# Third-norm parts of six late row blocks: stored in the attention stage, loaded for their products

## The reference

```
x = x + 0.5 * ffn(layernorm(x))
x = x + attention(layernorm(x))
x = x + 0.5 * ffn(layernorm(x))

def ffn(x):                       # x: tokens x 1024
    dots = softmax(x @ centroids.T / 0.1)          # 64 clusters
    hits = dots > 0.01
    query_sel, cluster_sel = any(hits, axis=1), any(hits, axis=0)
    dense = x @ weight.T + bias                    # 1024 x 1024
    return where(query_sel[:, None] & cluster_sel[assignments][None, :], dense, 0)
```

## Time and profile before

| | us |
|---|---|
| median of 3 runs | 1193.3 (1192.45 to 1193.41) |
| profiled execution, its own time | 1196.15 |
| its span | 1194.3 |
| TensorE busy | 1181.7 (99%) |
| VectorE busy | 799.3 (67%) |
| ScalarE busy | 499.2 (42%) |
| GpSimd busy | 441.0 (37%) |

### The profile page before, as it was taken

The page is one execution under the profiler, slowest core; times in us unless marked ns, Lnnn a source line. Parts: engine busy times, 40 slices in busy tenths (PEclk is TensorE's granted clock), DMA queues, the critical chain, the costliest instruction groups (busy, mean ns, idle before and its releaser), DMA issues.

```text
span 1194.3 us, 24986 instructions
## 1 busy us (share of the span) xinstructions
PE 1181.7 (99%) x10072; PEld 1002.5 (84%) x10072; DVE 799.3 (67%) x1272; ACT 499.2 (42%) x718; POOL 441.0 (37%) x582
## 2 busy tenths in 40 slices
PE   7999999999999999999999999999999999999998
PEld 6888888888888888888888888888888878888887
DVE  6654554455444477787777877778777774199987
ACT  5232233222211355656656656565565663211110
POOL 1335445543424643433434334344343210051332
PEclk9999999999999999999999999999999999999999
DMA  8578777876565366565565666565655565017885
GB/s 275 144 206 232 207 206 193 225 211 182 164 189 159 98 169 169 148 171 146 160 166 139 181 152 152 160 155 164 161 142 164 129 169 193 2 72 259 279 304 195
DMA packets 344978, 208.73 MB, mean 175 GB/s; under 512 B 289440, under 2 KB 308640, under 8 KB 344864
## 3 DMA queue, kind: packets, MB, share of 16 engines
q1 hardware_dynamic: 329696, 187.73, 56.2%
q10 hardware_dynamic: 15168, 19.40, 4.7%
HBM read 118.49 MB, written 88.60 MB: 173 GB/s over the span
## 4 chain that ended last, share of the span: by engine, by line
PE 91%; DMA 3%; DVE 2%; issue 1%; ACT 1%; SPq 1%; POOL 1%; POOLq 0%; DVEq 0%
PE ps_b L285 9%; PE ps_q L285 8%; PE ps_q L287 8%; PE ps_q L286 8%; PE ps_b L287 8%; PE ps_b L286 8%; PE ps_a L285 8%; PE ps_a L287 8%; PE ps_a L286 8%; PE ps_t L292 6%; PE ps_q L1450 3%; PE ps_q L299 2%; PE ps_q L301 2%; PE ps_q L1425 2%; DMA y_scratch<-xa 1%
## 5 line engine op out<-in xcount | busy, mean ns | idle before, releaser
L318 POOL TENSOR_TENSOR var_eps<-moments,eps 128x1 f32<-128x1 f32 x96 | 18.2, 190 | 396.6 <-DVE moments L314 396.6
L285 PE MATMUL ps_a<-w_hi,odd_hi 128*128 128x512 f32 x368 | 147.7, 401 | 0.0
L287 PE MATMUL ps_a<-w_hi,odd_lo 128*128 128x512 f32 x368 | 143.8, 391 | 0.0
L286 PE MATMUL ps_a<-w_lo,odd_hi 128*128 128x512 f32 x368 | 143.2, 389 | 0.0
L635 POOL TENSOR_SCALAR f_out<-f_out,token_on 128x1024 f32<-128x1024 f32 x30 | 85.6, 2852 | 75.6 <-DVE f_out L1013 75.3
L686 POOL TENSOR_TENSOR x_ring<-x_ring,f_tmp 128x1024 f32<-128x1024 f32 x32 | 77.3, 2414 | 91.2 <-DVE best L1159 58.5
L285 PE MATMUL ps_b<-proj_hi,y_hi 128*128 128x512 f32 x256 | 103.3, 403 | 0.0
L287 PE MATMUL ps_b<-proj_hi,y_lo 128*128 128x512 f32 x256 | 100.0, 391 | 0.0
L286 PE MATMUL ps_b<-proj_lo,y_hi 128*128 128x512 f32 x256 | 99.7, 390 | 0.0
L327 ACT ACTIVATE y_tok<-x_ring,norms 128x1024 f32<-128x1024 f32 x64 | 79.7, 1245 | 38.0 <-ACT o_head L881 21.0
L737 POOL TENSOR_TENSOR late<-late,mask 128x1024 f32<-128x1024 f32 x18 | 44.1, 2463 | 137.3 <-DMA late<-x_scratch 91.6
(11 more groups left out here) (219 smaller groups left out, 3113.1 us busy)
## 6 DMA issues: line engine op xcount, KB each, us to landing
xa<-in_L_attn_x SPq DMA_DIRECT2D x32, 512.0 KB, 5.0
f_tmp<-f_scratch SPq DMA_DIRECT2D x32, 512.0 KB, 4.2
x_ring<-in_L_attn_x SPq DMA_DIRECT2D x32, 512.0 KB, 3.6
f_scratch<-f_out SPq DMA_DIRECT2D x30, 512.0 KB, 4.0
x_scratch<-x_ring SPq DMA_DIRECT2D x30, 512.0 KB, 3.5
y_scratch<-xa SPq DMA_DIRECT2D x28, 512.0 KB, 4.6
ya_tok<-y_scratch SPq DMA_DIRECT2D x112, 128.0 KB, 3.3
late<-x_scratch SPq DMA_DIRECT2D x22, 512.0 KB, 6.7
```

The source lines that it names most:

```text
L285: pe.matmul(acc, hi[:, k, :], w_h[:, k, cols], start=(k == 0), stop=False)
L286: pe.matmul(acc, hi[:, k, :], w_l[:, k, cols], start=False, stop=False)
L287: last = pe.matmul(acc, lo[:, k, :], w_h[:, k, cols], start=False, stop=(k == KB - 1))
```

## The change

Six late blocks, v = 3, 5, 7, 9, 11 and 13 (blocks 9, 13, 17, 21, 25 and 29), are no longer normed, turned and split in the late stage. Their high and low parts, which the attention stage makes anyway for the logits, are stored to a new scratch tensor there, and loaded into the places of `late_set` in the late stage, after the block that used the place before. The semaphores count turned blocks (`TURNED`: v = 1, 2, 4, 6, 8, 10, 12) instead of all. x2 of the loaded blocks is still loaded, as the residual.

```diff
+    LOADED = list(range(3, len(LATE), 2))
+    TURNED = [v for v in range(1, len(LATE)) if v not in LOADED]
+    parts_d = nc.dram_tensor("parts_scratch", (len(LOADED), 2, P, KB, P), F32, kind="Internal").ap()
...
+        parts_stored, parts_in = w_in[6], [w_in[7], assign_in]
...
+                def store_parts(v):
+                    sp.wait_ge(lo3, LATE[v] + 1)
+                    for n, part_of in enumerate(third_set(LATE[v])):
+                        sp.dma_start(parts_d[LOADED.index(v), n], part_of.bitcast(F32)).then_inc(parts_stored, 16)
...
                     if 0 <= i - 4 < NT - 2:
                         store_x2(i - 4)
+                    if i - 5 in LATE[1:] and LATE.index(i - 5) in LOADED:
+                        store_parts(LATE.index(i - 5))
...
+                def load_parts(v):
+                    n = LOADED.index(v)
+                    sp.wait_ge(parts_stored, 32 * n + 48)
+                    for h in range(2):
+                        sp.wait_ge(ffnl[h], v - 2)
+                    for m, part_of in enumerate(late_set(v)):
+                        sp.dma_start(part_of.bitcast(F32), parts_d[n, m]).then_inc(parts_in[n % 2], 16)
...
                     if 7 <= v + 4 < NL:
                         load_late(v + 4)
+                    if v + 3 in LOADED:
+                        load_parts(v + 3)
...
                 def high_third(t):
                     act.wait_ge(t3, t + 1)
+                    if t - 2 in LATE[1:] and LATE.index(t - 2) in LOADED:
+                        act.wait_ge(parts_stored, 32 * LOADED.index(LATE.index(t - 2)) + 48)
                     act.copy(third_set(t)[0], ps_t[:, :, :]).then_inc(hi3, 1)
...
                 for v in range(3, NL):
-                    high_late(v)
+                    if v in TURNED:
+                        high_late(v)
                     if v == 3:
                         store_late(0)
-                    if v + 1 < NL:
+                    if v > 3 and v + 1 in TURNED:
                         norm_late(v + 1)
...
-                    if v > 0:
-                        dve.wait_ge(yl, v)
+                    if v in LOADED:
+                        dve.wait_ge(late_in[(v - 1) % 6], 16 * ((v - 1) // 6 + 2))
+                    elif v > 0:
+                        dve.wait_ge(yl, TURNED.index(v) + 1)
...
-                low_late(3)
                 for v in range(1, NL):
                     if v > 1:
                         read_late(v - 1, 1)
                         add_late(v - 1, 1)
-                        if 4 < v + 1 < NL:
+                        if v + 1 > 4 and v + 1 in TURNED:
                             low_late(v + 1)
...
+                    elif v in LOADED:
+                        n = LOADED.index(v)
+                        pe.wait_ge(parts_in[n % 2], 32 * (n // 2) + 48)
                     else:
-                        pe.wait_ge(lol, v)
+                        pe.wait_ge(lol, TURNED.index(v) + 1)
...
                 for v in range(2, NL):
-                    if v + 1 < NL:
+                    if v + 1 in TURNED:
                         transpose_late(v + 1)
                     product_late(v, 0)
                     product_late(v, 1)
```

More of the change, by code:

```diff
@@ L860, in norm_late @@
                         act.wait_ge(heads, NT)
-                    wait(act, tl, v - 2)
-                    normed(act, late_y[v % 2][:, :], late_slot(v)[:, :], 2, LATE[v]).then_inc(yl, 1)
+                    n = TURNED.index(v)
+                    wait(act, tl, n - 1)
+                    normed(act, late_y[(n + 1) % 2][:, :], late_slot(v)[:, :], 2, LATE[v]).then_inc(yl, 1)
                 def high_late(v):
-                    act.wait_ge(tl, v)
+                    act.wait_ge(tl, TURNED.index(v) + 1)
                     act.copy(late_set(v)[0], ps_t[:, :, :]).then_inc(hil, 1)
@@ L956, in _ @@
                 high_late(2)
-                norm_late(3)
+                norm_late(4)
                 select_mask(act, 1)
@@ L1098, in low_late @@
                     hi, lo = late_set(v)
-                    dve.wait_ge(hil, v)
+                    dve.wait_ge(hil, TURNED.index(v) + 1)
                     dve.tensor_tensor(lo, ps_t[:, :, :], hi.bitcast(F32), ALU.subtract).then_inc(lol, 1)
@@ L1393, in transpose_late @@
                 def transpose_late(v):
-                    pe.wait_ge(yl, v)
-                    if v == 1:
+                    n = TURNED.index(v)
+                    pe.wait_ge(yl, n + 1)
+                    if n == 0:
                         pe.wait_ge(lo3, NT)
                     else:
-                        pe.wait_ge(lol, v - 1)
-                    transposes(pe, late_y[v % 2]).then_inc(tl, 1)
+                        pe.wait_ge(lol, n)
+                    transposes(pe, late_y[(n + 1) % 2]).then_inc(tl, 1)
                 def product_late(v, h):
```

## The result

The change made the kernel slower: 1196.77 us at the median of 17 runs (1193.66 to 1200.05) against 1194.09 of 17 runs before (1192.45 to 1198.01), a ratio of 1.0024 with an interval of 1.0015 to 1.0032. The forecast was 1187.4 us. The profiled execution has a span of 1197.5 us, 3.2 more than that of before.

What follows compares the result with a forecast made beforehand. TensorE was taken to bound the kernel: 5.4 us of turns and 0.45 us of VectorE's lateness give 5.9 us less than 1193.3, so 1187.4 us, range 1186.3 to 1190.9 us.

Steps and rivals of the forecast that it cites:

- What bounds the kernel: Whole kernel: TensorE's instruction stream, busy 1181.7 of 1194.3 us, sets the end, with VectorE 0.45 us behind it.
- What the turns are worth: Late stage: six turns leave TensorE at 0.90 us each, 5.4 us in all, plus 0.45 us of VectorE's lateness.
- The attention stage taken at nothing: Attention stage: the stores of parts fit into SP's 4.7 us wait before the x load, so they cost nothing.
- rival C: Gain eaten: late stage at 1192.6 us, or attention stage losing 1 us in six steps; 1191 to 1195 us, chance 0.10.
- rival D: Attention stage: stores delay loads leading to q and k; slower from 1.4 us per pair, 1202 us at 2.5; chance 0.07.
- price of the pieces: DMA time of parts moved in 512-byte pieces: 1.5 to 2.5 us per 512 KB.
- Does the streamed chain hold?: Late stage: the streamed blocks' cycle falls from 23.59 to 22.0 us, under TensorE's new 22.67 us.
- the next one or two streams: Late stage: part loads delay only these streamed loads, by up to 3 us, with 2.4 us in hand.
- Which VectorE makes up in the following block: Late stage: the delay of up to 3 us is recovered through VectorE's shorter wait for the mask.
- B: Late stage: the streamed chain becomes the bound because the DMA engines need over 22.67 us; likely 1189.6 us, chance 0.20.
- the signs that I had set for being wrong: End chain running through streamed loads, or 512-byte pieces costing more than 2.5 us per 512 KB.
- the DMA share of the late blocks: Late stage, profile after: DMA engines' busy share over two late blocks at 0.95 or more.

Runs made afterwards that it cites:

- run without transfers: Kernel before with six late blocks neither turned nor loaded, no stores or loads of parts, so wrong numbers are multiplied: ratio 0.9951 to before, 5.8 us faster.
- products ahead: The change with parts laid out in 4 KB runs and each streamed block's product loaded one step before its x2: ratio 0.9953 to before, 5.6 us faster.
- late half alone: The change without stores of parts, its late loads taking other data of the same size: ratio 0.9995 to the kernel before.
- stores-only kernel: Kernel before plus only the attention stage's twelve stores of parts in 512-byte pieces and their guarding wait: ratio 1.0044 to before, 5.2 us slower.
- stores twice: Kernel before plus only the stores of parts in 512-byte pieces, each part stored two times: ratio 1.0189 to before, 22.6 us slower.
- whole rows: The change with the two places of the parts one after the other, so 4 KB runs instead of 512 bytes: ratio 0.9978 to before, 2.6 us faster.
- all three edits: The change with 4 KB runs, product parts loaded one step ahead, and stores of parts issued before the x2 store: ratio 0.9961 to before.

## Why the prediction was wrong
**What bounds the kernel**: right. TensorE's stream set the end but for 0.45 us, and the two things to watch were named.

**What the turns are worth**, 5.4 us and 0.45 more: right. The run without transfers has 5.8.

**The attention stage taken at nothing**: this step failed. I followed what stands behind the stores on SP's queue and their order, and found the x load on time, which it was. I left out the store of o_head, which another queue issues in the middle of the transfer and which SP waits for before o_tok. The step stood in the trace of before, though not in the rows I took from it: from 560 to 980 us SP's wait for it was 19.6 us in 22 waits. The cost was 5.2 us by the timed runs (1.0044), where the sum has nothing; I had kept up to 6 us as a part of rival C (0.10), and given a price above 1.4 us per pair, rival D, 0.07. The price of the pieces, 1.5 to 2.5 us per 512 KB, was not far off: the second store of a pair landed 7.5 us after its issue in pieces and 5.8 in rows, medians of six, so 0.85 us per store. What failed is where this time lies.
```profile
parts_scratch<-odd_lo SPq DMA_DIRECT2D x6, 512.0 KB, 7.5
```
```profile
parts_scratch<-odd_lo SPq DMA_DIRECT2D x6, 512.0 KB, 5.8
```

**Does the streamed chain hold?** This step failed too, and cost about as much: 5.3 us (0.9995 with the late loads of parts, 0.9951 without). I said its cycle falls from 23.59 to 22.0 us; it was 23.44 and 24.35. There were two faults. I took the loop by the one load that was critical before, and counted the missing subtraction as gone from the chain. There are two such loops, and the other one, whose load comes after the streamed block that stands alone between two late ones (not in a pair), keeps its subtraction, for the even block is still turned. And I let the parts delay only "the next one or two streams", with 2.4 us in hand. The stream that became critical is the next one behind the parts: its load took 7.13 and 7.68 us (6.33 and 5.74 in the chain of before). The parts had been issued 9 us before it, and the later of each pair landed 1.9 and 0.6 us after its issue, so they explain this delay only in part; which other transfer held it up is not shown. "Which VectorE makes up in the following block" did not come true, as the following load starts from its store.

**The rivals.** B has the place: VectorE idle before each mask and a last read far behind TensorE, as foreseen. Its reason is not the right one. I priced it by DMA engines with over 22.67 us of work; with 0.98 busy the kernel with products ahead is at its fastest, so it was not capacity but latency in a closed loop. Nor was TensorE wholly free of it, as I had said: it waited 0.5 and 0.2 us in the late stage. D has the sign for the attention stage and the right kind of mechanism, but at 0.9 us per pair, not 1.4 or more; only with the late loss beside it does the kernel get slower. The sum from the parts: −5.8 (turns) + 5.2 (stores in pieces) + 5.3 (late loads) = +4.7 us, and +2.9 measured. The difference is no more than the two intervals allow (the stores alone are known to 2 us, the late half alone to 2.3). That the two losses overlap, since a TensorE that starts the late stage later gives the streamed chain part of the time it lacks, would fit, but is not shown.

**The sum and the range**: the two losses were each known as a possibility with a chance of 0.2 and 0.07, and treated as apart. Together they put the time beyond the range. Of the signs that I had set for being wrong, the chain at the end did run through streamed loads; the DMA share of the late blocks, expected at 0.95 or more, was 0.91.

**What stays open.** The profiled execution of the stores-only kernel shows 2.6 us of waits, and the timed runs lost 5.2 us by their ratio. What the other half is was not seen. The clock may be a part of it: behind waits of 2.0 to 3.8 us it fell in the run with stores twice, and three of the six timed runs of stores only have a mean clock of 0.998 or 0.999; but one of 1201.63 us has 1.00. The width of the late half's runs (12 us) goes with the clock as well: 0.996 over 1200 us is 9.6 us at the lower level, an estimate, and in the profiles of the change, of whole rows and of the late half that level lies behind the last matmul. (The profiled execution of the change has 0.997, and its span ends 8.2 us behind its last matmul.) So the late half's long runs may be those in which VectorE ends last by far, but none of them was profiled. Open too is whether whole rows mend a third of the late loss.

## What to carry to other kernels
A store that "fits into a wait" of its own queue can still be in the way of a small transfer of another queue; before adding one, list every transfer in flight until it lands (here 8 us) and who waits for it. In a loop of load, work, store, load over a few buffers, look at every phase of the loop, not only the one that is critical now, and free each buffer from waits it doesn't need: here the product needed no store to be through. Lay data out in long runs before paying for its transfer: the same bytes cost 5.2 us or nothing. And count a wait of TensorE at more than its length where the clock falls behind it: in the run with stores twice this cost some 1.7 us more each of five times, after waits of 2.0 to 3.8 us.

## What the runs showed of the hardware
A store of 128 KB on ScalarE's queue took 7.7 us instead of 3.3 from its issue to the next transfer that waited for it, when 1 MB in 512-byte pieces had been issued 2.6 to 3.2 us earlier on SP's queue; the two stores of 128 KB in front of it landed in 6.7 us instead of 3.3.

The DMA engines sustained 346 GB/s at a busy share of 0.98 over 71 us (361 at 0.98 in the run with all three edits) without harm to a kernel whose loads were issued early enough, and 332 GB/s at 0.92 went with a loss where they were not.

TensorE's granted clock was 0.50 for some 3.4 us behind four of the five waits for k_mask in the run with stores twice (2.2 to 3.8 us), and stayed at 1.00 behind those of the change (0.2 to 0.8 us).
